# The order of score products and of a unit's heads in a cross-attention kernel: both halves of the rows in each unit, scores two batches ahead

## The reference

```
h   = layernorm(x);  q, k, v = h @ Wqkv + b;  ka, va = ctx @ Wqkv_aux + b   (16 heads of width 8)
out = softmax(q k^T / sqrt(8)) v * (1 - gate) + softmax(q ka^T / sqrt(8)) va * gate
x   = x + tanh(g_xattn) * (out @ Wo + bo)
h   = layernorm(x);  route each row to 8 of 64 experts (sigmoid scores, 4 of 8 groups, weights * 2.5)
x   = x + tanh(g_ffn) * (sum_e w_e * down_e(silu(gate_e(h)) * up_e(h)) + shared expert)
```

## Time and profile before

| what | us |
|---|---|
| median of 3 runs (lowest, highest) | 892.98 (892.52, 897.17) |
| the profiled execution's own time | 898.08 |
| its span in the trace | 896.3 |
| TensorE busy in the span | 849.5 (95%) |
| VectorE, ScalarE, GpSimd busy | 683.8, 562.4, 644.2 |

### The profile page before, as it was taken

The page is one execution under the profiler, slowest core; times in us unless marked ns, Lnnn a source line. Parts: engine busy times, 40 slices in busy tenths (PEclk is TensorE's granted clock), DMA queues, the critical chain, the costliest instruction groups (busy, mean ns, idle before and its releaser), DMA issues.

```text
span 896.3 us, 20102 instructions
## 1 busy us (share of the span) xinstructions
PE 849.5 (95%) x6765; PEld 660.1 (74%) x6765; DVE 683.8 (76%) x1652; ACT 562.4 (63%) x963; POOL 644.2 (72%) x605
## 2 busy tenths in 40 slices
PE   5899999989997899999999999999999999999997
PEld 3466666666665577888888888887888888888885
DVE  6888888878887747867867966976877776786665
ACT  4477778768776556557557557556656656655554
POOL 2567878877874247778777877787788777787775
PEclk9999999999999889999999999999999999999999
DMA  5577677686672055554654755654554645554652
GB/s 133 171 181 178 176 191 178 179 192 161 163 189 51 20 130 128 132 141 108 162 131 107 176 126 127 143 147 109 145 143 118 163 121 133 132 140 125 139 141 60
DMA packets 113619, 125.24 MB, mean 140 GB/s; under 512 B 27936, under 2 KB 75936, under 8 KB 112080
## 3 DMA queue, kind: packets, MB, share of 16 engines
q1 hardware_dynamic: 110640, 123.43, 55.2%
q10 hardware_dynamic: 2880, 0.59, 0.4%
HBM read 103.52 MB, written 19.96 MB: 138 GB/s over the span
## 4 chain that ended last, share of the span: by engine, by line
PE 78%; ACT 6%; DVE 4%; DMA 4%; issue 4%; POOL 1%; SPq 1%; ACTq 1%; POOLq 0%; DVEq 0%
PE bank L1918 19%; PE bank L1920 19%; PE bank L1919 19%; PE bank L1300 5%; PE bank L1287 4%; PE bank L1274 2%; ACT prob L787 2%; PE bank L1244 1%; DMA stack_k<-k_scratch 1%; PE bank L1321 1%; PE bank L1308 1%; DMA k_scratch<-parts_k 1%; ACTq L781 1%; POOL hid L1621 1%; PE bank L1250 1%
## 5 line engine op out<-in xcount | busy, mean ns | idle before, releaser
L1621 POOL TENSOR_TENSOR hid<-act,cwb 128x512 f32<-128x512 f32 x264 | 430.1, 1638 | 139.1 <-DVE act L1836 93.2
L1836 DVE TENSOR_TENSOR act<-silu,bank 128x512 f32<-128x512 f32 x264 | 180.2, 683 | 142.0 <-ACT silu L1670 134.7
L1670 ACT ACTIVATE silu<-bank 128x512 f32<-128x512 f32 x264 | 157.5, 597 | 208.6 <-PE bank L1920 208.2
L1918 PE MATMUL bank<-xhi,weights_hi 128*128 128x512 f32 x528 | 210.2, 398 | 0.0
L1920 PE MATMUL bank<-xlo,weights_hi 128*128 128x512 f32 x528 | 207.7, 393 | 0.0
L1919 PE MATMUL bank<-xhi,weights_lo 128*128 128x512 f32 x528 | 207.4, 393 | 0.0
L1840 DVE TENSOR_TENSOR hlo<-hid,hhi 128x512 fp32r<-128x512 f32 x264 | 199.7, 757 | 1.5 <-ACT hhi L1675 1.4
L985 DVE TENSOR_REDUCE mx<-bank 128x4 f32<-128x512 f32 x256 | 167.7, 686 | 30.0 <-PE bank L1274 24.1
L787 ACT ACTIVATE prob<-bank 128x1024 f32<-128x1024 f32 x128 | 130.9, 1022 | 77.9 <-PE bank L1287 76.2
L1675 ACT ACTIVATE hhi<-hid 128x512 fp32r<-128x512 f32 x264 | 164.7, 624 | 6.1 <-POOL hid L1621 5.5
L1920 PEld LDWEIGHTS bank<-xlo,weights_hi 128*128 128x128 f32 x528 | 99.3, 188 | 22.4
(11 more groups left out here) (227 smaller groups left out, 1009.5 us busy)
## 6 DMA issues: line engine op xcount, KB each, us to landing
cwb<-wts_scratch SPq DMA_DIRECT2D x176, 384.0 KB, 5.4
stack_k<-k_scratch SPq DMA_DIRECT2D x30, 384.0 KB
k_scratch<-parts_k SPq DMA_DIRECT2D x15, 384.0 KB, 3.4
stack_q<-q_scratch SPq DMA_DIRECT2D x30, 192.0 KB
k_scratch<-parts_k SPq DMA_DIRECT2D x15, 256.0 KB, 4.2
q_scratch<-parts_q SPq DMA_DIRECT2D x15, 192.0 KB, 2.4
xin<-in_x_dram SPq DMA_DIRECT2D x16, 128.0 KB, 2.3
cin<-in_ctx_dram SPq DMA_DIRECT2D x16, 128.0 KB, 2.6
```

The source lines that it names most:

```text
L1621: pool.tensor_tensor(h_buf[k][:], a_buf[k][:], cwb[slot][:, q % GP, :], ALU.mult).then_inc(h_ok, 1)
L1670: act.activation(s_buf[k % RS][:], g_bank[k % 2][:], ACT.Silu).then_inc(s_ok, 1)
L1836: nc.vector.tensor_tensor(a_buf[k % RS][:], s_buf[k % RS][:], u_bank[k % 3][:], ALU.mult).then_inc(a_ok, 1)
L1918: nc.tensor.matmul(bank, w[0], mh, start=first, stop=False)
```

## The change

A unit's four heads now come from both halves in turn (`head_of`), and go to the bank of their half; the probabilities are read from the matching places. A round issues its eight shifted products first, then four score products (`round_of_scores`) that alternate between the halves, each half with a bank of its own. Scores run exactly two batches ahead. `minus_max` therefore stands at the start of a batch, ahead of all its maxima. `out_proj` goes ahead of the `weighted` of its round. In the last body the projection of V goes to its regular place, and steps of the first routing are placed a little later.

```diff
@@ DVE
-        def maxima(b, par, u):
-            wait(dve, s_mm, UNITS * b + u + 1)
-            if u == 0:
+        def maxima(b, par, r, f):
+            wait(dve, s_mm, 2 * (ROUNDS * b + r) + f + 1)
+            if r == 0 and f == 0:
                 wait(dve, nm_ok, b - 1)
-            f, h = S_HEAD[u] // HH, S_HEAD[u] % HH
-            nc.vector.tensor_reduce(mx[par][:, 2 * f:2 * f + 2, h:h + 2].rearrange("p a h -> p h a"),
-                                    s_bank[u % 2][:].rearrange("p (h a k) -> p h a k", h=2, a=2),
+            nc.vector.tensor_reduce(mx[par][:, 2 * f:2 * f + 2, 2 * r:2 * r + 2].rearrange("p a h -> p h a"),
+                                    s_bank[f].rearrange("p (h a k) -> p h a k", h=2, a=2),
                                     AXX, ALU.max).then_inc(mx_ok, 1)
...
                 for u in range(UNITS):
-                    if u + AHEAD < UNITS:
-                        if one_more:
-                            maxima(b + 1, 1 - odd, u + AHEAD)
-                    elif two_more:
-                        maxima(b + 2, odd, u + AHEAD - UNITS)
-                    if u == UNITS - AHEAD - 1 and one_more:
+                    if u == 0 and one_more:
                         minus_max(b + 1, 1 - odd, min(n + 3 + odd, NC))
+                    if two_more:
+                        maxima(b + 2, odd, u // 2, u % 2)
                     if u == 1 and one_more:
                         evac_nmax(b + 1)
+                    if u == 1 and odd and n + 4 < NC:
+                        norm_mean(n + 4)
...
-                    if u == 7 and not odd and n + 4 < NC:
-                        norm_mean(n + 4)
-                    if last and k == 0 and u == 7:
+                    if last and k == 1 and u == 1:
                         first_lo()
@@ PE
+        def head_of(r, j):
+            f, e = j % 2, j // 2
+            return HH * f + 2 * (r ^ f) + e
+
+        def scores(b, r, e, f):
             n, c, s = b // CH, b % CH, b // CH % NST
-            if (c == 0 or n == 0) and j == 0 and u in (0, 3):
+            if (c == 0 or n == 0) and r == 0 and e == 0:
                 if n == 0:
-                    wait(pe, stk0[h // HH][c], 32)
+                    wait(pe, stk0[f][c], 32)
                 else:
-                    wait(pe, stk[h // HH][s], 32 * ((n - 1) // NST + 1 if s else n // NST))
+                    wait(pe, stk[f][s], 32 * ((n - 1) // NST + 1 if s else n // NST))
...
-            if j == 0:
-                wait(pe, mx_ok, UNITS * b + u - 1)
+            if e == 0:
+                wait(pe, mx_ok, 2 * (ROUNDS * b + r) - 1 + f)
...
+        def round_of_scores(b, r):
+            for e in range(2):
+                for f in range(2):
+                    scores(b, r, e, f)
...
                     for u in (2 * r, 2 * r + 1):
-                        shifted(b, u, 0)
-                        if ahead:
-                            scores(*ahead, 0)
-                        shifted(b, u, 1)
-                        shifted(b, u, 2)
-                        if ahead:
-                            scores(*ahead, 1)
-                        shifted(b, u, 3)
+                        for j in range(HPU):
+                            shifted(b, u, j)
+                    if two_more:
+                        round_of_scores(b + 2, r)
...
+                    if r == 3 and not first:
+                        out_proj(b - 1, 1 - odd)
                     for u in (2 * r, 2 * r + 1):
                         if u >= LAG:
                             weighted(b, odd, u - LAG, n, i)
...
-                    if (odd, r) == ((1, 2) if last else (0, 0)) and more:
+                    if (odd, r) == (0, 0) and more:
...
-                    if r == 3 and not first:
-                        out_proj(b - 1, 1 - odd)
...
-                    if last and k == 1 and r == 0:
+                    if last and k == 1 and r == 1:
                         first_logits()
-                    if last and k == 3 and r == 1:
+                    if last and k == 3 and r == 2:
                         first_turn_w()
```

More of the change, by code:

```diff
@@ L884, in body @@
                             first_xT()
-                    if last and k == 1 and r == 1:
+                    if last and k == 1 and r == 2:
                         first_exp()
@@ L888, in body @@
                         norm(3)
-                    if (odd, r) == ((1, 3) if last else (0, 1)) and more:
+                    if (odd, r) == (0, 1) and more:
                         if first:
@@ L902, in body @@
                         first_gate()
-                    if last and k == 3 and r == 2:
+                    if last and k == 3 and r == 3:
                         first_wT()
@@ L1176, in on_dve @@
         for u in range(UNITS):
-            maxima(0, 0, u)
+            maxima(0, 0, u // 2, u % 2)
         minus_max(0, 0, 3)
         evac_nmax(0)
-        for u in range(AHEAD):
-            maxima(1, 1, u)
+        for u in range(UNITS):
+            maxima(1, 1, u // 2, u % 2)
             if u == 4:
@@ L1279, in shifted @@
         def shifted(b, u, j):
             n, c = b // CH, b % CH
[L1281 removed]
+            a, r = u % 2, u // 2
+            f, e, at_half = j % 2, j // 2, head_of(r, j) % HH
             if u == 0 and j == 0:
                 wait(pe, shift, 16 * (b + 1))
[L1284 to L1288 removed]
+            if j == 0 and a == 0:
+                wait(pe, p_ok, ROUNDS * b + r)
@@ L1335, in first_turn_x @@
             pe.wait_ge(fg_ev, 1)
+            pe.wait_ge(v_ev, NC)
             pe.wait_ge(fxn_ok, 2)
@@ L1376, in on_pe @@
         transposes(2, 0)
-        for u in range(UNITS):
-            scores(0, u, 0)
-            scores(0, u, 1)
+        for r in range(ROUNDS):
+            round_of_scores(0, r)
         pe.wait_ge(v_ev, 1)
@@ L1382, in on_pe @@
         turn_max(0)
-        for u in range(AHEAD):
-            scores(1, u, 0)
-            scores(1, u, 1)
-            if u == 3:
+        for r in range(ROUNDS):
+            round_of_scores(1, r)
+            if r == 1:
                 project_ka(2, 0)
```

43 lines of the change are left out of this document (16 added, 27 removed).

## The result

The changed kernel takes **904.06 us** (median of four runs, 903.04 to 906.06) beside 892.75 for the kernel before (four runs, 892.05 to 897.17): ratio 1.0119, 95% interval 1.0081 to 1.0157. Measured once more in a later comparison it stood at 1.0096 (1.0073 to 1.0119). It is slower, inside the range on record, 5 us above the forecast of 898.7. The profiled execution took 906.06 us with a span of 904.3, 8.0 more than the span of before.

The account below looks back on a forecast made before the run. TensorE, busy 95% of the span, was taken as the bound, with four engines nearly full in attention. Terms 0 + 7.3 + 4.3 - 5.9 = +5.7 us turned 898.1 into 903.8, the median 892.98 into 898.7; range 888 to 907.

Parts of the forecast that it names:

- Parts 1 and 2: Rounds: reordered columns gain TensorE nothing; the exponential starts 0.24 us earlier but gains 0 a body, bounds 0 to 0.9.
- rival (d): The halves do not run side by side: 0.22 us more in 120 rounds, 26 us, 925; chance 0.02.
- (a): Half 0 of the stack keeps up and no wait arises: 877 us at best, 884 with half; chance 0.15.
- Part 3: Steady bodies: scores wait 1.2 us for half 0, body 17.2 instead of 16.74; 7.3 us lost, 5 to 10.7.
- rival (b): New waits lower TensorE's clock: six of them at about 1.1 us each, 905 us; chance 0.14.
- Part 4: Prologue: gaps between pairs of maxima and a later start delay batches 0 and 1; 4.3 us lost, bounds 1 to 5.
- Part 5: Last body to first expert product: idle gap and part of the low-clock cost go; 5.9 us saved, bounds 2.5 to 9.

Follow-up runs that it names:

- experiment 1: The kernel before, with both halves of a stack waited for at a batch's first score unit, nothing else changed: 908.93 us, ratio 1.0135.
- experiments 2 and 8: Both on the changed kernel. 2: GpSimd's weight remainders behind the splits, ratio 1.0039. 8: scores seven rounds ahead instead of eight, ratio 1.001.
- experiment 4: The changed kernel with the prologue's score products of batches 0 and 1 issued bank by bank: 906.43 us, ratio 1.0104.
- section 11: The kernel with scores seven rounds ahead, plus SyncE's load of k waiting for VectorE's copy of the turned maxima: 889.87 us, ratio 0.9914.

## Why the prediction was right, and where it was off

**Parts 1 and 2, columns and exponential: right.** That the halves run side by side shows in batch 30, where eight shifted products stand without scores: alternating between the halves they take 0.40 us, where the earlier trace rows had 0.62 in one half.

```profile
302.68 0.40 PE L1291 MATMUL bank<-stack_q,stack_k 64*128 64x128 bf16 x8
```

So rival (d) falls; (a) falls with the waits for k. A body without a wait takes 16.52 us for 16.74, 0.2 of the 0.9 that were its bound, and round 2 still waits 0.65 us for the exponential. The reason given, that the issue of the shift rows holds ScalarE back in round 0, fits the kernels that issue them a round later: the pause is gone there. That these also changed the place of the maxima keeps this short of a proof.

**Part 3, half 0 of the stack: right mechanism, too small.** The first score of an even batch's round 0 waits for the load of k, as the text on record said; experiment 1 shows that this alone makes the loss, experiments 2 and 8 that it goes when k comes earlier or is wanted later. The forecast had 7.3 us. Measured are 13.6 beside the undisturbed kernel before (10.8 with its accident), more than its longest numbers were said to give (10.7; worked out again by its own loop, these give some 12.8, and the shortest 5.6 for 5). The waits are 13.0 us in 7, some 1.9 each instead of 1.2, in every second body or so, and the bodies are long and short in turn as the text allowed. Four things had a wrong size. First the landing: half 1 and half 0 were taken at 5.5 + 1.6 = 7.1 us from the start of SyncE's issue. In the changed kernel's chain, and in SyncE's timeline, the longest of them stands so:

```profile
158.52 7.63 DMA stack_k<-k_scratch
```

```profile
157.72 1.55 SPq L430 DMA_DIRECT2D stack_k<-k_scratch  x2
```

The chain counts the flight of half 0 from the start of its own issue, the second, 0.80 us behind the first; from the first it is 8.4 us here. By the landings that the trace records, half 0 of all fifteen stacks took 7.0 to 8.4 us from the first issue, 7.5 in the median (7.1 to 8.2 and 7.3 in the kernel before). Second, the loop: from the scores at 129.22 to those at 166.19 it is 37.0 us where 34.4 was worked out, and the two loops behind it take 36.1 each, the fourth 34.1. In the first three the load was issued 28.4 to 28.6 us behind the scores, some 1.2 later than the 27.3 of the forecast (27.85 less 0.3 and less 0.25). One of the three had the full clock throughout, so the clock is not the whole reason; the rest of it stays open. Third, the low clock: rival (b) stood apart from the forecast with its own chance, six waits at 1.1 us; it was two waits and 3.1 us, on top of part 3. Fourth, waits for the shift rows (3.0 us in 4) were in no term.

**Part 4, the prologue: too large, and mostly for the wrong reason.** 2.6 us instead of 4.3. The pattern is there, two maxima and a gap:

```profile
23.75 1.29 DVE L982 TENSOR_REDUCE mx<-bank 128x4 f32<-128x512 f32 x2 [0.70 <-PE bank L1272]
25.53 1.29 DVE L982 TENSOR_REDUCE mx<-bank 128x4 f32<-128x512 f32 x2 [0.49 <-PE bank L1272]
...
29.10 1.29 DVE L982 TENSOR_REDUCE mx<-bank 128x4 f32<-128x512 f32 x2 [0.50 <-PE bank L1272]
```

The eight of batch 0 take 6.64 us (23.75 to 29.10 + 1.29) instead of the 5.52 of the earlier trace rows: 1.1 more, where the text had 2.0: a pair takes 1.29 where two single maxima were put at 1.38, and the gap of some 0.5 stands three times between the pairs, not four. But these gaps hardly reach TensorE. Experiment 1 has the old order and its maxima in one block (5.27 us), and its batch 2 starts as late as in the changed kernel; experiment 4 takes the gaps away and wins 0.5 us. What moves the prologue is half 0 again, of the second stack, for which the scores in batch 0 wait. The text named this load only as a cover, with half 1 landed at 36.56; half 0 lands at 38.7, 2.1 us later. That a sum of other terms came near the 2.6 is luck.

**Part 5, the last body: right, and a cover missed.** 7.0 us gained until the first expert product for a forecast of 5.9; alone, in the old order, 6.7. The turn of the routing weights one round later was costed at nothing, since 12 us of gate and up products stand ahead of the first down product, with 1 to 2 us if that cover were gone. It was gone: the first down product waits 2.72 us, and this part ends 1.6 us worse (2.5 where the last body's edits stand alone). The cover had been counted against one round, not against all that the first down product waits for. The store of the routing weights is issued 1.35 us ahead of the first expert product, before it was 3.87; the broadcast weights come 5.90 us after their issue, and that stands behind the store of 2.02 and the turn.

```profile
324.32 2.02 DMA wts_scratch<-f_wT
326.36 0.67 SPq L557
327.08 5.90 DMA cwb<-wts_scratch
```

**The sum** was right in sign and low. For the profiled execution it gave 903.8 and 906.06 came, 2.3 more: +3.5 in part 3, -1.7 in part 4, -1.1 in part 5, +1.6 in the experts. That part 4's excess made up for half of part 3's lack is luck. On the medians it is 5.4 low, because the median of before lay 5.1 us under its profiled execution and that of the changed kernel only 2.0 under its own. The profiled execution of before holds the accident of 2.8 us, which the forecast left in its base; without it the stretches give 10.8 us, and the medians lie 11.3 apart.

What stays open: why the load of k was issued 1.2 us later in the loop than worked out, and what part of the gain in section 11 the kernel before could have had with the same wait in its own order. Its trace has one wait for the shift rows, 2.0 us, the accident.

## What to carry to other kernels

An operand that is loaded in pieces has a deadline for each piece. A reordering that is neutral in products can move one of them: list, for each piece, when it lands and when its first reader stands, before counting columns. Where a wait closes a loop through other engines, it comes back, and a low clock behind it can be part of its price: here behind two waits of seven.

When a wait is cured, look for the small transfer next to the large one. Here 16 KB that were issued less than a microsecond behind 768 KB held TensorE for 13.4 us, and one wait ahead of the large one's issue turned a ratio of 1.001 into 0.9914.

## What the runs showed of the hardware

A small transfer on one queue suffers from a large one on another, and which of them is issued first decides how much. In the kernel with the scores seven rounds ahead the shift rows (16 KB, ScalarE's queue) are issued 0.34, 0.56 and 0.88 us behind the load of k (768 KB, SyncE's queue) at batches 10, 14 and 16, and its chain of waits has them fly 5.99, 4.92 and 6.58 us, counted from the start of the issue. The first of them:

```profile
119.50 5.99 DMA stack_q<-nmaxT
```

The traces also record when each transfer has landed, waited for or not. From 45 us on, for the shift rows that are issued within 3 us of a load of k, counted from the start of their issue:

| kernel | issued, against the load of k | rows | landed after, us |
|---|---|---|---|
| before | 0.1 to 0.7 us ahead | 5 | 2.0 to 3.2 |
| seven rounds ahead | 0.2 to 2.9 us behind | 13 | 4.8 to 6.6 |
| before | 0.2 to 0.9 us behind | 8 | 4.8 to 7.6 |
| section 11 | in the same instant (one 1.1 us ahead) | 14 | 2.0 to 2.9 |

The accident of the kernel before is the 7.59 of the earlier trace rows: its load of k had been issued 0.95 us ahead of the rows' 183.40.

```profile
182.45 1.55 SPq L432 DMA_DIRECT2D stack_k<-k_scratch  x2
```

In the earlier trace rows, in the same kernel, the rows are issued at 133.15 and k at 133.36, and the rows landed after 2.43 us. Ahead of the load the rows' first packet starts 1.3 us after their issue, behind it 2.6 to 5.6 us; so most of the delay lies before their first packet. What holds them there the traces do not tell. The Trainium skill (DMA: Bandwidth & Descriptors, Queues, rings and completion order) says that each transfer engine goes round the queues that it has work for, packet by packet. That rule alone does not say that the order of two issues should count for 3 us; these landings say that it does.

The place of a transfer that nobody waits for mattered as well. Moved behind the load of k (1.023) or ahead of the loads of x (1.0093 where 1.0039 was), the expert weights made the kernel slower both times. In the traces another transfer is then waited for longer: the shift rows in the one, the context of x in the other.
